# Attention stage: the value copy, the running sums and the update of X in other places, the normalised chunk on GpSimd

## The reference

```python
x = x + 0.5 * _L0_ffn_ref(_layernorm(x, axis=-1), ...)
x = x + _L0_attn_ref(_layernorm(x, axis=-1), L0_attn_Wq, L0_attn_Wk, L0_attn_Wv)
x = x + 0.5 * _L0_ffn_ref(_layernorm(x, axis=-1), ...)
```

```python
q, k, v = x @ Wq.T, x @ Wk.T, x @ Wv.T       # shortened
fk = jnp.fft.rfft(k, axis=-1); fk = fk / (jnp.abs(fk) + EPS)
fq = jnp.fft.rfft(q, axis=-1); fq = fq / (jnp.abs(fq) + EPS)
fv = jnp.fft.rfft(v, axis=-1)
fkv = jnp.cumsum(fk * fv, axis=-2)
values_hat = jnp.fft.irfft(fkv * jnp.conj(fq), n=D, axis=-1)
return x + values_hat
```

## Time and profile before

| | |
|---|---|
| median of 3 runs | 1613.17 us (1612.79 to 1613.87) |
| profiled execution | 1618.11 us, span 1616.1 us |
| PE busy | 1433.0 us, 89% |
| DVE busy | 1282.3 us, 79% |
| ACT busy | 940.4 us, 58% |
| GpSimd busy | 787.2 us, 49% |
| mean granted clock of PE | 0.969 of full speed |

### The profile page before, as it was taken

One profiled execution on the slowest core, in us unless ns is written; L12 is line 12 of the kernel. 1 busy time (PEld: TensorE's weight loads), 2 busy tenths in 40 slices (PEclk: granted clock), 3 DMA queues, 4 the chain that ended last, 5 costly groups with the idle time before them and its releaser, 6 DMA issues.

```text
span 1616.1 us, 34769 instructions
## 1 busy us (share of the span) xinstructions
PE 1433.0 (89%) x9656; PEld 1283.5 (79%) x9657; DVE 1282.3 (79%) x3425; ACT 940.4 (58%) x1435; POOL 787.2 (49%) x992
## 2 busy tenths in 40 slices
PE   0899999998999998799998977999999998999994
PEld 0677777777999998798888865777777787999994
DVE  4688888876789997677779975887888876799996
ACT  4344333333777775888888892443333335888883
POOL 0344554443676666443334322445544432766764
PEclk9999999999999999999999987999999998999997
DMA  8511111114577775100001010111111115688887
GB/s 286 159 52 51 54 54 54 47 47 135 153 222 228 232 229 162 46 1 1 0 0 52 26 40 21 40 49 54 54 54 47 48 64 150 182 254 268 269 270 229
DMA packets 108284, 177.01 MB, mean 110 GB/s; under 512 B 13936, under 2 KB 73208, under 8 KB 107896
## 3 DMA queue, kind: packets, MB, share of 16 engines
q1 hardware_dynamic: 82280, 104.16, 22.8%
q0 software_dynamic: 25920, 71.86, 12.0%
HBM read 95.75 MB, written 86.70 MB: 113 GB/s over the span
## 4 chain that ended last, share of the span: by engine, by line
DVE 24%; PE 22%; issue 21%; DMA 10%; ACT 10%; POOL 8%; DVEq 3%; SPq 2%; ACTq 1%; POOLq 0%
PE bank L721 6%; DMA lists<-a_rows,a_slots 6%; PE bank L723 6%; PE bank L722 6%; POOL lists L438 6%; DMA b_xb<-lists 2%; ACT a_rows L556 2%; DVE b_yb L1268 2%; PE bank L870 2%; DVE a_gate_u L1131 2%; DVE X L1280 2%; DVEq L1248 2%; DVE X L1340 1%; DVE X L1323 1%; DVE t_fq L1375 1%
## 5 line engine op out<-in xcount | busy, mean ns | idle before, releaser
L450 POOL DMA_INDIRECT results<-b_yb,b_goal x284 | 328.5, 1157 | 191.7 <-issue 104.3
L438 POOL DMA_INDIRECT lists<-a_rows,a_slots x256 | 256.6, 1002 | 148.2 <-POOL a_rows L431 53.0
L507 ACT ACTIVATE a_uh<-a_gate_u 128x512 fp32r<-128x512 f32 x128 | 77.0, 625 | 228.8 <-PE bank L723 196.1
L721 PE MATMUL bank<-a_sw2h,a_uh 128*128 128x256 f32 x512 | 154.4, 302 | 54.1 <-DVE a_xtl L1004 41.4
L721 PE MATMUL bank<-b_xbth,b_w1h 128*128 128x256 f32 x568 | 171.5, 302 | 0.0
L721 PE MATMUL bank<-ew_h,b_hth 128*128 x568 | 160.3, 282 | 0.0
L723 PE MATMUL bank<-b_xbth,b_w1l 128*128 128x256 f32 x568 | 160.2, 282 | 0.0
L722 PE MATMUL bank<-b_xbtl,b_w1h 128*128 128x256 f32 x568 | 160.0, 282 | 0.0
L723 PE MATMUL bank<-ew_h,b_htl 128*128 x568 | 159.1, 280 | 0.0
L722 PE MATMUL bank<-ew_l,b_hth 128*128 x568 | 158.9, 280 | 0.0
L525 ACT ACTIVATE a_gate_u<-bank 128x512 f32<-128x512 f32 x128 | 75.9, 593 | 128.3 <-DVE a_ul L1004 76.2
(11 more groups left out here) (214 smaller groups left out, 4788.4 us busy)
## 6 DMA issues: line engine op xcount, KB each, us to landing
b_xb<-lists SPq DMA_DIRECT2D x142, 264.0 KB
b_yt<-results SPq DMA_DIRECT2D x112, 256.0 KB
X<-in_L_attn_x SPq DMA_DIRECT2D x16, 512.0 KB, 4.5
out<-X SPq DMA_DIRECT2D x16, 512.0 KB, 4.2
results<-b_yb,b_goal POOLq DMA_INDIRECT x284
lists<-in_c_fill SPq DMA_DIRECT2D x16, 264.0 KB, 4.0
w_raw_ew<-in_L_ffn_ew SPq DMA_DIRECT2D x2, 2048.0 KB, 13.8
lists<-a_rows,a_slots POOLq DMA_INDIRECT x256, 2.4
```

The source lines that it names most:

```text
L438: pool.indirect_dma_start(out=lists, out_offset=bass.IndirectOffsetOnAxis(ap=slots[:, q, k, j:j + 1], axis=0), in_=rows[:, q, j, :], in_of ...
L450: pool.indirect_dma_start(out=results, out_offset=bass.IndirectOffsetOnAxis(ap=goal[:, u, blk:blk + 1], axis=0), in_=YB[:, u % 4, blk, :], ...
L507: return act.activation(o, i, ACT.Copy)
L721: pe.matmul(o, a("h"), b("h"), start=first, stop=False)
```

## The change

GpSimd, instead of ACT, writes XN: one multiplication with rstd and one addition of shift, each over 128x1024, after its sum of Q's squares and after the transposes of the chunk before. ACT copies VT ahead of the FK copy instead of behind the first logarithm. PE makes the running sums before the transposes of XN. DVE takes the three products with the running sums ahead of XA["l"], and the addition to X moves by one step: the values of chunk s-2 are added in step s, between FQ's sums and its multiplication by RB (P).

```diff
--- before.py
+++ after.py
@@ -54,7 +54,7 @@
 HM = NF - 1
 TINY = 1e-30
 
-DVE_A, DVE_T, POOL_T, ACT_T = 86, 28, 16, 8
+DVE_A, DVE_T, POOL_T, ACT_T = 86, 28, 18, 8
 
 
 C_ID, C_TRI, C_ONE, C_RESE, C_RESJ = 0, 128, 256, 384, 416
@@ -493,6 +493,15 @@
                 if now:
                     pool.wait_ge(s_qev, s + 1)
                     power_sum(J).then_inc(s_qsum, 1)
+                if far and not (isinstance(s, int) and s < 0):
+                    atleast(pool, s_atp, s + 2)
+                    ch.settle()
+                    apart(pool)
+                    ch.link(pool.tensor_tensor(XN[:], X[:, bass.ds((s + 2) * J, J), :],
+                                               rstd[:, par, :].unsqueeze(2).broadcast_to([P, J, D]), ALU.mult))
+                    ch.settle()
+                    pool.tensor_tensor(XN[:], XN[:], shift[:, par, :].unsqueeze(2).broadcast_to([P, J, D]),
+                                       ALU.add).then_inc(s_txn, 1)
 
             run_steps(pool, attention, -2, 4, CH - 2, CH, 2, ch, POOL_T)
             step_a = steps_a(1)
@@ -639,6 +648,11 @@
                 if now:
                     act.wait_ge(s_kps, s + 1)
                     act.activation(SQ[:, 0:J], kq_ps, ACT.Square).then_inc(s_ksq, 1)
+                if inside(s - 2, CH):
+                    act.wait_ge(s_ptp, s - 1)
+                    atleast(act, s_aps, s * 2 - 4)
+                    copy(VT[:], bank[:, 0:2, :]).then_inc(s_ph, 1)
+                if now:
                     atleast(act, s_kvd, s)
                     copy(FK[:], kq_ps).then_inc(s_kev, 1)
                 if now or prev:
@@ -649,10 +663,6 @@
                         act.wait_ge(s_qsum, s)
                         atleast(act, s_p, s - 1)
                     ca.link(act.activation(inverse, power, ACT.Ln, bias=tiny[:, 0:1]))
-                if inside(s - 2, CH):
-                    act.wait_ge(s_ptp, s - 1)
-                    atleast(act, s_aps, s * 2 - 4)
-                    copy(VT[:], bank[:, 0:2, :]).then_inc(s_ph, 1)
                 if now or prev:
                     ca.settle()
                     ca.link(act.activation(inverse, inverse, ACT.Exp, scale=0.5))
@@ -672,10 +682,6 @@
                     ca.link(act.activation(inverse, inverse, ACT.Ln, bias=fft_eps[:, 0:1]))
                     ca.settle()
                     act.activation(inverse, inverse, ACT.Exp, scale=-1.0).then_inc(s_root, 1)
-                if far:
-                    act.wait_ge(s_rstd, s + (CH + 3))
-                    atleast(act, s_atp, s + 2)
-                    normalised(s + 2, par, XN)
 
             shared_weights(0)
             router_weights()
@@ -947,10 +953,6 @@
                     if isinstance(s, int) and s == 0:
                         pe.wait_ge(s_mlo, 6)
                     spectrum(2, 2).then_inc(s_qps, 1)
-                if nxt:
-                    pe.wait_ge(s_txn, s + 2)
-                    atleast(pe, s_ph, s - 1)
-                    transposed(XN_FIRST[1] if isinstance(s, int) and s == 0 else XN)
                 if prev:
                     pe.wait_ge(s_kvd, s)
                     pe.wait_ge(s_px, s)
@@ -963,6 +965,10 @@
                         if before[j] is not None:
                             ins = pe.matmul(o, ones_f, before[j], start=False, stop=True)
                     ins.then_inc(s_cps, 1)
+                if nxt:
+                    pe.wait_ge(s_txn, s + 2)
+                    atleast(pe, s_ph, s - 1)
+                    transposed(XN_FIRST[1] if isinstance(s, int) and s == 0 else XN)
                 if old:
                     if isinstance(s, int) and s == 2:
                         pe.wait_ge(s_inv, 16)
@@ -1311,18 +1317,21 @@
             def attention(s, par, half, meanwhile=None):
                 prev, now, nxt, far = inside(s - 1, CH), inside(s, CH), inside(s + 1, CH), inside(s + 2, CH)
                 lo, hi = slice(1, NF), slice(NF + 1, D)
-                if inside(s - 3, CH):
-                    at = 0 if isinstance(s, int) and s == CH + 2 else 4
-                    dve.wait_ge(s_txn, s - 2)
+
+                def attended(c, at):
+                    dve.wait_ge(s_txn, c + 1)
                     for h in range(2):
-                        dve.wait_ge(s_aps, s * 2 + (h - 5))
+                        dve.wait_ge(s_aps, c * 2 + (h + 1))
                         apart(dve)
                         for i in range(2):
-                            t = s * J + (2 * h + i - 3 * J)
+                            t = c * J + (2 * h + i)
                             xt = X[:, bass.ds(t, 1), :].rearrange("p a d -> p (a d)")
                             ins = dve.scalar_tensor_tensor(xt, xt, rstd_1[:, bass.ds(t, 1)],
                                                            bank[:, at + h, i * D:(i + 1) * D], ALU.mult, ALU.add)
                         ins.then_inc(s_aout, 1)
+
+                if isinstance(s, int) and s == CH + 2:
+                    attended(CH - 1, 0)
                 if prev:
                     dve.wait_ge(s_root, s)
                     atleast(dve, s_cps, s - 1)
@@ -1361,22 +1370,26 @@
                     ch.link(dve.tensor_tensor(FK[:, :, lo], FK[:, :, lo], FK[:, :, hi], ALU.subtract))
                     ch.settle()
                     ch.link(dve.tensor_tensor(FK[:, :, hi], TA[:], TB[:], ALU.add))
+                if prev:
+                    c_ps, fq = bank[:, 6:8, :].rearrange("p b (j d) -> p (b j) d", j=2), FQ[:, 1 - par]
+                    ch.settle()
+                    dve.wait_ge(s_cps, s)
+                    dve.wait_ge(s_qev, s)
+                    ch.link(dve.tensor_tensor(TA[:], c_ps[:, :, lo], fq[:, :, hi], ALU.mult))
+                    ch.link(dve.tensor_tensor(TB[:], c_ps[:, :, hi], fq[:, :, lo], ALU.mult))
+                    ch.settle()
+                    dve.tensor_tensor(fq, c_ps, fq, ALU.mult).then_inc(s_cused, 1)
                 if nxt:
                     dve.wait_ge(s_ah, s + 2)
                     low(XA["l"][:], bank[:, 0:2, :], XA["h"][:]).then_inc(s_al, 1)
                 if prev:
-                    c_ps, fq = bank[:, 6:8, :].rearrange("p b (j d) -> p (b j) d", j=2), FQ[:, 1 - par]
-                    ch.settle()
-                    dve.wait_ge(s_cps, s)
-                    dve.wait_ge(s_qev, s)
-                    ch.link(dve.tensor_tensor(TA[:], c_ps[:, :, lo], fq[:, :, hi], ALU.mult))
-                    ch.link(dve.tensor_tensor(TB[:], c_ps[:, :, hi], fq[:, :, lo], ALU.mult))
-                    ch.settle()
-                    dve.tensor_tensor(fq, c_ps, fq, ALU.mult).then_inc(s_cused, 1)
                     dve.wait_ge(s_cused, s)
                     ch.link(dve.tensor_tensor(fq[:, :, lo], fq[:, :, lo], fq[:, :, hi], ALU.add))
                     ch.settle()
                     ch.link(dve.tensor_tensor(fq[:, :, hi], TB[:], TA[:], ALU.subtract))
+                if inside(s - 2, CH) and (prev or not isinstance(s, int)):
+                    attended(s - 2, 4)
+                if prev:
                     ch.settle()
                     dve.wait_ge(s_root, s + 1)
                     ch.link(dve.tensor_tensor(fq[:, :, 0:NF + 1], fq[:, :, 0:NF + 1], RB[:, J:], ALU.mult))
@@ -1409,7 +1422,6 @@
                 return step
 
             step_a = attention(CH, 0, CH // 2, next_layer)
-            attention(CH + 1, 1, CH // 2)
             step_a(-2, 0, -1)
             step_a(-1, 1, -1)
             attention(CH + 2, 0, CH // 2 + 1)
```

More of the change, by code:

```diff
@@ L1363, in attention @@
                     ch.link(dve.tensor_tensor(FK[:, :, hi], TA[:], TB[:], ALU.add))
-                if nxt:
-                    dve.wait_ge(s_ah, s + 2)
-                    low(XA["l"][:], bank[:, 0:2, :], XA["h"][:]).then_inc(s_al, 1)
                 if prev:
@@ L1375, in attention @@
                     dve.tensor_tensor(fq, c_ps, fq, ALU.mult).then_inc(s_cused, 1)
+                if nxt:
+                    dve.wait_ge(s_ah, s + 2)
+                    low(XA["l"][:], bank[:, 0:2, :], XA["h"][:]).then_inc(s_al, 1)
+                if prev:
                     dve.wait_ge(s_cused, s)
```

## The result

The changed kernel takes 1628.95 us, the median of four runs (1626.75 to 1634.32), against 1613.10 before: a ratio of 1.0102, 95% interval 1.0077 to 1.0128, some 16 us slower. Two later sets of runs gave 1.0096 (1.0078 to 1.0113) and 1.0074 (1.0058 to 1.0091). The forecast was slower by 28 us, 1641. It lies where rival B had put it (1625 to 1633), and near rival C's 1632.

The account below looks back on a forecast made before the run. A ring of waits through ACT and DVE (19.93 us a step) was the bound, DVE itself in steps 10 to 13. Terms +12.2, +10.0, -0.5, -1.5, -1 made +19, with the clock +28: 1641 us, range 1612 to 1656.

Parts of the forecast that it names:

- rival B: Rival, chance 0.24: XN delays t_fq's sum, but P comes before the t_sq sum; ring 20.4, total 1625 to 1633 us.
- rival C: Rival, chance 0.20: both collisions, but TensorE's clock is kept; +19 us, 1632.
- both collisions: GpSimd holds DVE twice a step: XN's second operation delays t_fq's sum (2.0 us lost), the t_sq sum delays P.
- steps 2 to 10: Nine attention-stage periods at +1.35 us each (21.28 against 19.93), +12.2 in all, before the clock.
- the second collision: On DVE, P is asked for at C + 8.8 and waits for GpSimd's t_sq sum to C + 9.7; ring 21.28 us.
- the low clock: TensorE drops to 1.2 GHz behind its 3.8 us gap, slowing V and Q: 0.9 us in ten steps, +9, bounds 0 and +15.
- The ring without exclusion: Chain of waits per attention step if GpSimd and DVE never block each other: 18.45 us, 1.5 under 19.93.
- XN's price: GpSimd's two 128x1024 operations at 2.38 us each, 4.86 with the gap between; bounds 1.2 and 3.0 each.
- Steps 10 to 13: DVE-bound steps: 2.3 to 2.4 us lost to XN, 0.2 at P; +2.5 a step, +10.0 in all.
- First and last steps: Step 1, still filling, -0.5 us; last period, with no XN left, -1.5; earlier X update before the next stage, about -1.
- Rival A: Rival, chance 0.14: no collision, XN's operations under 1.4 us each or broadcast operand not taking the port; faster, 1600 us.

Follow-up runs that it names:

- e5: The changed kernel as it is, run again as a measure for others on its chip: 1.0096 of the kernel before.
- e11: The changed kernel as it is, run once more as a measure on a later chip: 1627.38 us, 1.0074 of the kernel before.
- e10: The changed kernel with 20 extra matmuls a step in TensorE's gap ahead of the t_fq transposes: 1623.60 us, 1.0056 of the kernel before.
- e1: The changed kernel with t_xn made by ScalarE again, all reorderings kept: 0.9948 of the kernel before.
- e2: The changed kernel without GpSimd's second operation on t_xn (adding shift): 0.9957 of the kernel before.
- e7: The kernel before with two reorderings, c_ps products ahead of XA's low part and VT ahead of FK: 1604.31 us, 0.9939 of before.
- e12: The changed kernel with TensorE's transposes of t_xn ahead of the running sums again: 1.0020 of the kernel before.

## Why the prediction was right or wrong

The direction, the place and both collisions were right. The size was 12 us too large by the medians (+28 against +16), and 16.4 by the profiled executions, as the one of before was slow among its runs (1618.1 against 1613.1) and the changed one wasn't. Most of the excess is in steps 2 to 10, where the second collision and the low clock were summed as if they didn't bear on each other. From the first KV to the last the profile of before takes 293.8 us and that of the changed kernel 308.9, +15.1; that is the quickest of its three, as e5 and e11 take 314.8 and 312.7. With the clock kept (e10) it is 307.9, +14.1, where +20.7 was forecast without the clock.

**The ring without exclusion** (18.45): right. e1, e2 and e7 measured 18.32, 18.32 and 18.14.

**XN's price** (2 x 2.38): too high. The two operations took 1.89 each. The line through GpSimd's three sizes, taken as "the engine's own line", overstated this form by 0.49. XN ended 1.0 us earlier, so the wait of t_fq's sum was 1.25 to 1.5 and not 2.0, and P was asked for ahead of the t_sq sum and not inside it. Why the form is cheaper was not tried. That its rows lie in one piece is hardly the reason, as those of t_px (256 wide) do so too and lie on the line of t_sq (rows of 127); the broadcast operand is left. The estimate of 2.25 from the Trainium skill (GPSIMD Engine Reference, Elementwise — side-by-side cycle accounting) was nearer, and too high as well.

**The second collision** (P waits for the whole t_sq sum): half right. The two operations of P were counted as one. The t_sq sum slipped between them, so the first ran in 0.69 and only the second stood, 1.06 us more. And it wasn't in every step: in steps 3 to 9 it stood in two, six and three of seven in the changed kernel's profiles. The prediction had said that the two engines meet within 0.3 us.

**Steps 2 to 10** (+1.35 each, +12.2 in all, before the clock): too high. With the gap filled, at full clock, the steady steps took 20.3 and 20.6 in turn (e10) and not 21.28, and the nine periods +6.3 in all. Of the 1.0 us by which a step of 20.3 is shorter, 0.5 lies in P, which ended 10.4 us behind the running sums instead of 10.9, and 0.4 in TensorE's part of the ring, from P's end to the end of the running sums, which took 9.9 instead of 10.37 (both in the step before 810.12). The changed kernel itself, with its low clock, had +7.3, +14.3 and +9.9 in its three profiles, where the forecast with all of its clock term comes to about +21.

**Steps 10 to 13** (+10.0): right at +9.5, +8.5 and +9.1 in the three profiles, but with other shares: 1.2 on t_fq's sum (L1387 with 1.88 there) and 1.06 on P, not 2.3 and 0.2. Two errors met and cancelled, which was luck.

**The clock** (+9 in ten steps, bounds 0 and +15): the low clock came into most steps, as forecast, but behind gaps of 2.0 us too and not only of 3.3. The stage's profiles show 2.4, 4.4 and 10 us net in seven steps, and the medians of the runs, e11 less e10, 3.8. Its own price was near the forecast (some 7 to 10 in seven steps, an estimate). What was missed is that the second collision came in fewer steps beside it, so that the two don't add up. The bounds held. The kernel before also has a seventh gap of over 2 us that the prediction's count of six leaves out (2.81 us, before the transposes at 1001.21), with the low clock behind it like the others.

**First and last steps:** the first KV came 0.2 us later and not 0.5 earlier, and the first two periods, which stand in the nine above at +1.35 each, measured +1.1 together. -1.5 was forecast for the last period, and -1.7 measured over the last two. -1 was forecast at the handover; from the last KV to ScalarE's copy of the next stage's first transposes it took 21.9 us before and 19.2 after, -2.7.

Rival A (1600, no collision) named the right condition: under 1.4 us an operation. They took 1.89, and e2, which fulfils it by having one, came to -7 us where -13 was put: its steps 10 to 13 took 20.7 and not the 19.9 assumed. Rival B named the right period, 20.4, from a wrong pair: it left the second collision out and had XN at 2.38. Rival C, both collisions with the clock kept, is what e10 is: +9 us, where +19 was put. That the changed kernel came out near B and C is no sign for either, as both collisions and the low clock are in it.

## What to carry to other kernels

Before work is moved from ScalarE to GpSimd, lay its operations beside VectorE's with two SBUF operands, with times: an idle GpSimd is of no use if it holds VectorE just where VectorE is on the ring, and some 3 us of order on a third engine (e12) decide how much. VectorE's standing time by itself says nothing: in e2 it stands 1.1 us a step for free. A gain of a reordering shows only without the collision: the same reorderings gave -8.5 us without t_xn on GpSimd and +16 with it. And a wait that opens a gap of 2 to 3 us on TensorE can cost more than the gap, as here the clock fell behind most of them, and differently from run to run. Two such costs of one wait should not be summed before it is asked whether the one moves the other.

## What had not been expected

GpSimd's tensor_tensor of 128x1024 with a broadcast operand took 1.89 us, less per element (1.85 ns) than the 128x508 and 128x256 operations without one (2.5 and 2.9).

In all the fast versions steps 10 to 13 became longer than before (20.7 to 20.8 against 20.1). In e1 the t_sq sum meets the addition of the experts' results there, GpSimd first:

```profile
868.31 2.12 POOL L469 TENSOR_TENSOR t_sq<-t_sq 128x508 f32<-128x508 f32 x1 [6.89 <-ACT t_sq L641]
```

and the first of VectorE's eight operations:

```profile
869.21 1.50 DVE L1344 SCALAR_TENSOR_TENSOR X<-t_yg,gates,X 128x256 f32<-128x256 f32 x1
```

It takes 1.50 us, and all eight 5.85 where they take 4.81 in the changed kernel. Beside GpSimd's t_px operations, which have two SBUF operands as well, the others keep their pace of 0.6 us, and t_px takes 0.80 to 0.93 instead of 0.74. Why the one pair excludes each other and the other hardly does stays open.
